# Three of six exponentials read from their PSUM bank, and a new order of work on VectorE, ScalarE and GpSimd

## The chip, the cores and the metric

One core of a Trainium2 chip runs the whole program. The metric is the device time of one execution in microseconds (us), median of several runs. On the core five engines run side by side, each with its own list of instructions in a fixed order: TensorE (PE in the profile, its weight loads PEld), VectorE (DVE), ScalarE (ACT), GpSimd (POOL) and SyncE (SP), which issues DMAs. They order each other only through semaphores: an instruction adds to one when it is done, and another engine waits until it has reached a count.

## What is computed

The reference is a decoder of two layers over 16 sequences of 256 tokens with 256 features: differential attention, cross attention, a mixture of experts, then a state-space block, causal cross attention and a feed-forward block with low-rank additions. After each comes a residual sum and a layer normalisation. Only the state-space block is touched:

```
zxbcdt = einsum('bld,ed->ble', x, in_proj_w)                 # z, x, B, C and dt per token
xBC    = silu(conv over 4 tokens (x, B, C) + conv_b)
dt     = softplus(dt + dt_bias);  A = -exp(A_log)
step:    state = state * exp(A * dt_t) + (x_t * dt_t) B_t;   y_t = state . C_t     # 8 heads
y      = (y + x * D) * silu(z)
y      = y * rsqrt(mean(y * y) + eps) * norm_w
out    = layernorm(x + y @ out_proj_w)
```

## The kernel before

`state_space` handles one sequence of 256 tokens in each step `n`, and the loop `STEPS` runs from -7 to 16, so that several sequences are in flight: in step n the block's core runs for sequence n, the output of sequence n-1 is finished, and sequences n+4, n+5 and n+7 are normalised, summed from the experts' outputs and gathered. The input projection is made for two sequences at a time (a pair), six of its eleven units in even steps and five in odd ones, through two PSUM banks (`in_ps`). So even and odd steps differ, and each engine has a list of its own for each, written out by hand.

The scan over tokens is done as matrices. For each sequence there are three blocks of 128 x 128 tokens and eight heads, which makes six units `u` of four heads (`u // 2` is the block). For each:

- `exponents(n, u)` on TensorE sums the decays into one of two PSUM banks, `e_ps[u % 2]` (two matmuls, of the high and the low part of the rows);
- `decays(n, u)` on ScalarE (line 2670) takes the exponential and writes it to `mat[:, u]` in SBUF;
- `matrices(eng, n, u)` (line 2827) multiplies `mat[:, u]` by the masked products `gm` of B and C, in place. VectorE does units 0, 2 and 4, GpSimd 1, 3 and 5;
- `mix(n, blk)` on TensorE multiplies the matrices with the rows `xdt` and `xdt_tail`. Its first half needs VectorE's three units, the second GpSimd's.

TensorE may write a bank again for `exponents(n, u + 2)` when `decays(n, u)` has read it: it waits for `decay_ready`. The same banks take the turned rows of the next sequence in `to_rows`, which VectorE's `scaled_rows` (line 2955) reads before the next step's exponents.

Other names that the steps below use: `masked_products` makes `gm` (line 2939, PSUM times a constant); `taps` are the convolution's three later taps on VectorE (line 2893, three instructions a unit), after ScalarE's `first_tap`; they free a bank of `in_ps`. `high_terms` (line 2930) and GpSimd's `low_terms` (line 3127) make the rows that the next exponents sum, `rhs_hi` and `rhs_lo`. `sum_experts` (lines 2867 and 2874, then moments) adds what the experts made of a sequence that comes five steps later; GpSimd's `scale_x` makes a scale and a shift of its moments in four small instructions, and ScalarE's `normalize_x` applies them a step later. `mean_squares` (line 2962) takes the mean square of y, GpSimd's `scale_rows` (line 3120) its inverse root, `residual` (line 2971) uses that; `row_moments`, GpSimd's `scale_y` (lines 3097 to 3102) and ScalarE's `normalize_y` finish the sequence. `skip_terms`, `gated` (line 3002), ScalarE's `upper_y` and `square_y` and GpSimd's `split_y` (line 3137) lead to TensorE's `output` in the next step. `gather` (line 3089) issues four indirect DMAs from GpSimd. `copy_steps` takes the dt rows out of their bank on ScalarE for TensorE's `turn_steps`.

## Time and profile before

| | us |
|---|---|
| median of 3 runs (2669.08 to 2676.38) | 2672.24 |
| the profiled execution | 2671.63 |
| its span, first to last instruction | 2669.9 |
| steps 4 and 5 of the state-space stage, from 1749.5 us on | 50.0 |
| mean granted TensorE clock, share of full speed | 0.937 |

Over the span TensorE was busy for 88%, its weight loads 74%, VectorE 73%, GpSimd 61% and ScalarE 53%. The state-space stage with all 16 sequences lies between about 1650 and 2050 us. A row of a timeline tells the start, the length, the engine, the line, the output and the inputs; `x2` are two instructions in one row, and a bracket holds the engine's idle time before it and what ended that. Rows of consecutive instructions overlap by about 0.1 us, since the end of one is written while the next begins.

### The profile page before, as it was taken

The numbers are of one execution on the slowest core, as the hardware profiler recorded it, in microseconds if no ns is written. First come the engines' busy times: TensorE is split into PE (matmuls) and PEld (weight loads), VectorE is DVE, ScalarE is ACT, GpSimd is POOL, SyncE is SP. The second block draws the span as 40 slices with busy tenths as digits, with TensorE's granted clock in tenths as the row PEclk, the third lists the DMA queues.
The fourth block names the chain that finished last, engine by engine and source line by source line (L and its number), as shares of the span: only waits on it lengthen the run. The fifth ranks groups of instructions, "written<-read, shape, count | busy, mean of one in ns | idle before, by whom it ended". The sixth has DMA issues, their size and how long they took to land. (4 is left out here: it accounts for less than half of the span.)

```text
span 2669.9 us, 63255 instructions
## 1 busy us (share of the span) xinstructions
PE 2341.5 (88%) x23480; PEld 1968.6 (74%) x23480; DVE 1950.1 (73%) x3223; ACT 1423.5 (53%) x2223; POOL 1619.4 (61%) x1937
## 2 busy tenths in 40 slices
PE   5999999997799877998999965988995899987998
PEld 4677777775566656998999964777774666756998
DVE  2677777776589872646888857999984588875776
ACT  2566666664466652335666544655652466653333
POOL 3667666764467751275666656777764587863443
PEclk9899999999899987999999987998996799988999
DMA  8566666551889841146666652111002887841111
GB/s 205 131 159 159 160 145 158 153 120 43 245 216 229 219 111 36 52 138 204 224 228 226 230 175 64 41 48 32 21 13 85 213 225 208 224 105 41 53 54 52
DMA packets 227288, 363.44 MB, mean 136 GB/s; under 512 B 51968, under 2 KB 156416, under 8 KB 219520
## 3 DMA queue, kind: packets, MB, share of 16 engines
q1 hardware_dynamic: 207392, 281.32, 39.7%
q0 software_dynamic: 17376, 78.13, 8.6%
q8 instruction: 143, 2.34, 0.4%
q10 hardware_dynamic: 2304, 1.05, 0.2%
q14 instruction: 73, 0.60, 0.1%
HBM read 231.72 MB, written 133.69 MB: 137 GB/s over the span
## 5 line engine op out<-in xcount | busy, mean ns | idle before, releaser
L1369 ACT ACTIVATE self_probs<-self_score_ps 128x768 f32<-128x768 f32 x256 | 208.7, 815 | 183.9 <-PE self_score_ps L1271 182.0
L1585 POOL TENSOR_SCALAR_AFFINE_SELECT self_probs<-self_probs 128x512 f32<-128x512 f32 x256 | 169.5, 663 | 158.6 <-ACT self_probs L1369 158.6
L1506 DVE TENSOR_REDUCE self_neg_max<-self_max_ps 128x2 f32<-128x256 f32 x256 | 108.1, 422 | 165.1 <-PE self_max_ps L88 165.1
L647 ACT ACTIVATE cross_probs<-cross_score_ps 128x1024 f32<-128x1024 f32 x128 | 131.2, 1025 | 101.6 <-PE cross_score_ps L545 100.0
L745 DVE TENSOR_REDUCE cross_neg_max<-cross_max_ps 128x4 f32<-128x1024 f32 x128 | 154.9, 1212 | 39.1 <-PE cross_max_ps L524 39.0
L1507 DVE TENSOR_REDUCE self_neg_max<-self_max_ps 128x2 f32<-128x512 f32 x256 | 174.5, 682 | 0.0
L2297 POOL TENSOR_TENSOR moee_h_lo<-moee_h,moee_h_hi 128x512 fp32r<-128x512 f32 x78 | 112.5, 1442 | 92.3 <-ACT moee_h_hi L2034 91.6
L739 DVE TENSOR_REDUCE causal_block_max<-causal_max_ps 128x6 f32<-128x768 f32 x128 | 120.9, 946 | 56.4 <-PE causal_max_ps L88 55.9
L3592 POOL TENSOR_TENSOR ffn_g_lo<-ffn_g_full,ffn_g_hi 128x512 fp32r<-128x512 f32 x64 | 82.1, 1283 | 129.2 <-ACT ffn_g_hi L3478 116.9
L2034 ACT ACTIVATE moee_h_hi<-moee_h 128x512 fp32r<-128x512 f32 x110 | 69.6, 632 | 163.2 <-DVE moee_h L2200 163.2
L647 ACT ACTIVATE causal_probs<-causal_score_ps 128x768 f32<-128x768 f32 x128 | 103.6, 809 | 99.2 <-PE causal_score_ps L545 99.0
L79 PE MATMUL moee_g_ps<-moee_x_hi,moee_in_hi 128*128 128x256 f32 x440 | 131.3, 298 | 10.0 <-DVE moee_x_lo L2187 5.8
L1271 PE MATMUL self_score_ps<-self_q_stack,self_k_stack 49*128 49x128 f32 (+1 forms) x1024 | 129.0, 330 | 10.0 <-ACT self_probs L1369 6.4
L2200 DVE TENSOR_TENSOR moee_h<-moee_u_ps,moee_silu 128x512 f32<-128x512 f32 x110 | 75.5, 686 | 82.0 <-PE moee_u_ps L81 77.4
L2240 POOL DMA_INDIRECT x_tiles<-kept_x,moek_slot x64 | 65.8, 1029 | 107.1 <-issue 104.1
L79 PE MATMUL moee_y_ps<-moee_out_hi,moee_h_hi 128*128 128x256 f32 x440 | 125.4, 285 | 0.7 <-DVE moee_out_lo L2152 0.7
L81 PE MATMUL moee_g_ps<-moee_x_hi,moee_in_lo 128*128 128x256 f32 x440 | 125.7, 286 | 0.0
L79 PE MATMUL moee_u_ps<-moee_x_hi,moee_in_hi 128*128 128x256 f32 x440 | 125.7, 286 | 0.0
L80 PE MATMUL moee_g_ps<-moee_x_lo,moee_in_hi 128*128 128x256 f32 x440 | 125.7, 286 | 0.0
L80 PE MATMUL moee_u_ps<-moee_x_lo,moee_in_hi 128*128 128x256 f32 x440 | 125.1, 284 | 0.0
L81 PE MATMUL moee_u_ps<-moee_x_hi,moee_in_lo 128*128 128x256 f32 x440 | 125.1, 284 | 0.0
L81 PE MATMUL moee_y_ps<-moee_out_hi,moee_h_lo 128*128 128x256 f32 x440 | 124.9, 284 | 0.0
(507 smaller groups left out, 9479.9 us busy)
## 6 DMA issues: line engine op xcount, KB each, us to landing
self_q<-self_q_split SPq DMA_DIRECT2D x48, 512.0 KB, 3.5
self_q_raw<-self_q SPq DMA_DIRECT2D x32, 768.0 KB, 8.2
cross_stacks<-cross_qk SPq DMA_DIRECT2D x64, 384.0 KB, 6.4
causal_stacks<-causal_qk SPq DMA_DIRECT2D x64, 384.0 KB, 6.4
moe_y_tiles<-lasting_y_out SPq DMA_DIRECT2D x55, 256.0 KB, 2.5
mid<-lasting_y_out SPq DMA_DIRECT2D x48, 256.0 KB, 2.2
x_tiles<-zeros SPq DMA_DIRECT2D x16, 624.0 KB, 5.5
moee_xT<-x_tiles SPq DMA_DIRECT2D x39, 256.0 KB, 7.3
```

The source lines that it names most:

```text
L79: pe.matmul(out, a[0], b[0], start=start, stop=False, **kw)
L80: pe.matmul(out, a[0], b[1], start=False, stop=False, **kw)
L81: return pe.matmul(out, a[1], b[0], start=False, stop=stop, **kw)
L647: nc.scalar.activation(probs[i // 2][:, a, :, lo:], score_ps[:, :, lo:], ACT.Exp, scale=HD ** -0.5).then_inc(prob_ready, 1)
L739: last = dve.tensor_reduce(block_max[:, :, col % 4, :], bank[:, :, 0:3 * P].rearrange("p a (j t) -> p a j t", t=P), AX.X, ALU.max, negate= ...
L745: last = dve.tensor_reduce(neg_max[p][:, tile, :, col % 4, :], bank[:].rearrange("p a (q k) -> p a q k", q=QT), AX.X, ALU.max, negate=True)
L1271: last = pe.matmul(score_ps[:, ab, j * S + k * P:(j + 1) * S], k_stack[p][rows, tile, k * P:(k + 1) * P], q_stack[rows, 4 * tile + c, k * P:],
L1369: nc.scalar.activation(probs[g % 4][:, a, :, P:], score_ps[:, :, P:], ACT.Exp, scale=HD ** -0.5).then_inc(prob_ready, 1)
L1506: dve.tensor_reduce(neg_max[:, tile, :, c, 0:1], bank[:, :, 0:P], AX.X, ALU.max, negate=True)
L1507: dve.tensor_reduce(neg_max[:, tile, :, c, 1:2], bank[:, :, S:2 * S], AX.X, ALU.max, negate=True).then_inc(max_kept, 1)
L1585: pool.affine_select(diagonal, diagonal, [[0, 2], [0, 2], [1, P]], ALU.is_ge, zero, base=0, channel_multiplier=-1).then_inc(prob_masked, 1)
L2297: pool.tensor_tensor(h_lo[p][f][:].rearrange("p j s -> p (j s)"), h[f][:], h_hi[p][f][:].bitcast(F32).rearrange("p j s -> p (j s)"), ALU.s ...
```

## The change

Three things change in `state_space`; nothing else does.

1. `decays` of units 0, 2 and 4 write the exponential back into the bank `e_ps[0]` that they read, and VectorE's `matrices` reads it from there. So the bank is free only when VectorE has multiplied: `exponents` 2 and 4, and `to_rows` for its first half, wait for `low_mat_ready` in place of `decay_ready`. The wait for the earlier `mix`, which protects `mat`, moves to the first writer.
2. The order on VectorE. Even steps: the multiplications go between the taps, `sum_experts` from the start behind multiplication 4, `residual` to right behind `mean_squares`, `high_terms` behind `gated`. Odd steps: multiplications 0 and 2 follow `masked_products`, then `tail_rows`, taps, multiplication 4, `sum_experts`, `mean_squares`, `residual`.
3. ScalarE in even steps: `decays` 1 follows `decays` 0, `normalize_x` comes behind `decays` 3, `copy_steps` ahead of `square_y`. GpSimd in odd steps: `scale_x` comes behind multiplication 5, ahead of `low_terms`, not behind the gather.

```diff
             def exponents(n, u):
-                if u >= 2:
+                if u in (2, 4):
+                    pe.wait_ge(low_mat_ready, 3 * n + u // 2)
+                elif u >= 2:
                     pe.wait_ge(decay_ready, 6 * n + u - 1)
...
             def to_rows(b):
                 for q in range(QT):
-                    if b:
-                        pe.wait_ge(decay_ready, 6 * b - 1 + q)
+                    if b and q == 0:
+                        pe.wait_ge(low_mat_ready, 3 * b)
+                    elif b:
+                        pe.wait_ge(decay_ready, 6 * b)
...
             def decays(n, u):
                 act.wait_ge(e_done, 6 * n + u + 1)
-                if u == 0 and n:
+                if u == 1 and n:
                     act.wait_ge(ssm_done, 2 * n)
-                nc.scalar.activation(mat[:, u, :, :].rearrange("p h t -> p (h t)"), e_ps[u % 2][:],
-                                     ACT.Exp).then_inc(decay_ready, 1)
+                dst = mat[:, u, :, :].rearrange("p h t -> p (h t)") if u % 2 else e_ps[0][:]
+                nc.scalar.activation(dst, e_ps[u % 2][:], ACT.Exp).then_inc(decay_ready, 1)
...
         def matrices(eng, n, u, ready):
             eng.wait_ge(decay_ready, 6 * n + u + 1)
             eng.wait_ge(gm_ready, n + 1)
-            eng.tensor_tensor(mat[:, u, :, :], mat[:, u, :, :],
+            src = mat[:, u, :, :] if u % 2 else e_ps[0][:].rearrange("p (h t) -> p h t", t=P)
+            if u == 0 and n:
+                eng.wait_ge(ssm_done, 2 * n)
+            eng.tensor_tensor(mat[:, u, :, :], src,
                               gm[:, u // 2, :].unsqueeze(1).broadcast_to([P, 4, P]), ALU.mult).then_inc(ready, 1)
...
         # ScalarE, even steps
                     if now:
                         decays(n, 0)
+                        decays(n, 1)
                     first_tap(n, 1)
-                    if real(n + 4):
-                        normalize_x(n + 4)
                     if now:
-                        decays(n, 1)
                         decays(n, 2)
                         tails(n)
                         decays(n, 3)
+                    if real(n + 4):
+                        normalize_x(n + 4)
...
                     if now:
                         upper_y(n)
+                    copy_steps(n)
+                    if now:
                         square_y(n)
                     if late:
                         normalize_y(n - 1)
-                    copy_steps(n)
...
         # VectorE, even steps
+                    if now:
+                        masked_products(n)
+                        matrices(dve, n, 0, low_mat_ready)
+                    taps(n, 0)
+                    if now:
+                        matrices(dve, n, 2, low_mat_ready)
+                    taps(n, 1)
+                    if now:
+                        tail_rows(n)
+                        matrices(dve, n, 4, low_mat_ready)
                     if real(n + 5) and n != -2:
                         sum_experts(n + 5)
-                    if now:
-                        masked_products(n)
-                    taps(n, 0)
-                    taps(n, 1)
-                    if now:
-                        matrices(dve, n, 0, low_mat_ready)
-                        matrices(dve, n, 2, low_mat_ready)
-                        tail_rows(n)
-                    if n >= 0 and soon:
-                        high_terms(n + 1)
-                    if now:
-                        matrices(dve, n, 4, low_mat_ready)
                     taps(n, 2)
                     if late:
                         mean_squares(n - 1)
-                    taps(n, 3)
+                        residual(n - 1)
                     if now:
                         skip_terms(n, 0)
-                    if late:
-                        residual(n - 1)
+                    taps(n, 3)
                     if now:
                         skip_terms(n, 1)
                         gated(n)
+                    if n >= 0 and soon:
+                        high_terms(n + 1)
...
         # VectorE, odd steps
                         masked_products(n)
-                    if real(n + 5):
-                        sum_experts(n + 5)
-                    if now:
                         matrices(dve, n, 0, low_mat_ready)
                         matrices(dve, n, 2, low_mat_ready)
                         tail_rows(n)
                     taps(n, 0)
+                    if now:
+                        matrices(dve, n, 4, low_mat_ready)
+                    if real(n + 5):
+                        sum_experts(n + 5)
                     if late:
                         mean_squares(n - 1)
-                    if now:
-                        matrices(dve, n, 4, low_mat_ready)
-                    if late:
                         residual(n - 1)
...
         # GpSimd, odd steps
                         matrices(pool, n, 5, high_mat_ready)
-                    if n == -5:
-                        scale_x(n + 5)
-                    if n == -3:
+                    if n >= -5 and real(n + 5):
                         scale_x(n + 5)
...
                         gather(n + 7)
-                    if n >= -1 and real(n + 5):
-                        scale_x(n + 5)
```

## Rows read from the trace of the kernel before

**Rows 1.** Windows: stretch and length, busy time (instructions) of each engine, PEclk, DMA.
```profile
1749.50:1775.00 25.50, 20.98 (x148) 17.38 (x148) 24.71 (x41) 11.53 (x20) 17.23 (x22) 0.93 0.04 13
1775.00:1799.50 24.50, 22.80 (x160) 19.72 (x160) 23.28 (x50) 18.70 (x29) 21.20 (x19) 1.00 0.25 74
...
1902.00:1995.00 93.00, 85.25 (x594) 71.83 (x592) 83.12 (x139) 55.86 (x88) 57.26 (x54) 0.94 0.04 12
```

**Rows 2.** Groups by line on VectorE, 1652.8 to 1925.7: busy us, mean ns.
```profile
L2827 DVE TENSOR_TENSOR ssm_mat<-ssm_mat,ssm_gm 128x512 f32<-128x512 f32 x33 | 36.4, 1129 | 0.0
...
L2947 DVE TENSOR_TENSOR ssm_xdt_tail<-ssm_xdt,ssm_tail 128x512 f32<-128x512 f32 x11 | 11.8, 1076 | 0.0
```

**Rows 3.** Two lines over the whole span: ns minimum/median/maximum, first and last start.
```profile
L2827 DVE TENSOR_TENSOR ssm_mat<-ssm_mat,ssm_gm x48: 656/790/2387, 1658.3 to 2021.6; 128x512 f32<-128x512 f32 x48
...
L2955 DVE TENSOR_TENSOR ssm_xdt<-ssm_e_ps,ssm_dt x32: 656/681/691, 1646.1 to 2011.7; 128x512 f32<-128x512 f32 x32
```

**Rows 4.** Timeline of VectorE in steps 4 and 5: start, us, instruction.
```profile
1754.32 2.59 DVE L2827 TENSOR_TENSOR ssm_mat<-ssm_mat,ssm_gm 128x512 f32<-128x512 f32 x2
1756.84 1.77 DVE L2947 TENSOR_TENSOR ssm_xdt_tail<-ssm_xdt,ssm_tail 128x512 f32<-128x512 f32 x1
...
1763.62 0.15 DVE L2962 TENSOR_SCALAR ssm_ms<-ssm_g_ps 128x2 f32<-128x2 f32 x1
...
1775.46 1.91 DVE L2867 SCALAR_TENSOR_TENSOR ssm_y_shared<-ssm_y_routed,moek_weight,ssm_y_shared 128x256 f32<-128x256 f32 x2
...
1783.35 2.37 DVE L2827 TENSOR_TENSOR ssm_mat<-ssm_mat,ssm_gm 128x512 f32<-128x512 f32 x1
1786.40 0.88 DVE L2971 SCALAR_TENSOR_TENSOR lasting_y_out<-ssm_xT_ps,ssm_row_scale,ssm_x 128x256 f32<-128x256 f32 x2 [0.68 <-issue]
...
1793.76 3.01 DVE L2930 TENSOR_TENSOR ssm_rhs_hi<-ssm_triang,ssm_a_hi 128x1024 fp32r<-128x1024 f32 x2
1796.69 0.87 DVE L2867 SCALAR_TENSOR_TENSOR ssm_y_shared<-ssm_y_routed,moek_weight,ssm_y_shared 128x256 f32<-128x256 f32 x2
...
1799.47 0.52 DVE L2939 TENSOR_TENSOR ssm_gm<-ssm_g_ps,ssm_triang 128x384 f32<-128x384 f32 x1
```

**Rows 5.** Timeline of GpSimd in the same steps.
```profile
1754.64 3.42 POOL L2827 TENSOR_TENSOR ssm_mat<-ssm_mat,ssm_gm 128x512 f32<-128x512 f32 x2
...
1763.85 0.69 POOL L3120 TENSOR_TENSOR ssm_row_scale<-ssm_ms,ssm_neg_half 128x2 f32<-128x2 f32 x1 [1.23 <-DVE ssm_ms L2962]
...
1771.14 0.23 POOL L3097 TENSOR_SCALAR ssm_var<-ssm_mv 128x2 f32<-128x2 f32 x1 [2.89 <-issue]
...
1772.54 0.20 POOL L3102 TENSOR_TENSOR ssm_shift<-ssm_low,ssm_rstd 128x2 f32<-128x2 f32 x1
...
1777.25 1.09 POOL L3089 DMA_INDIRECT ssm_y_routed<-moe_y_tiles,moek_slot  x1 [0.17 <-issue]
...
1782.62 2.54 POOL L2827 TENSOR_TENSOR ssm_mat<-ssm_mat,ssm_gm 128x512 f32<-128x512 f32 x2
...
1788.46 1.90 POOL L3127 TENSOR_TENSOR ssm_rhs_lo<-ssm_triang,ssm_a_lo 128x1024 fp32r<-128x1024 f32 x1 [0.90 <-DVE ssm_a_lo L2924]
```

**Rows 6.** Timeline of ScalarE, end of step 5.
```profile
1792.74 1.09 ACT L2759 ACTIVATE lasting_y_out<-lasting_y_out,ssm_shift,ssm_rstd 128x256 f32<-128x256 f32 x2 [0.67 <-POOL ssm_shift L3102]
...
1798.70 0.60 ACT L2670 ACTIVATE ssm_mat<-ssm_e_ps 128x512 f32<-128x512 f32 x1
```

**Rows 7.** Timeline of TensorE in step 4, around its longest wait.
```profile
1749.54 0.39 PE L2526 MATMUL ssm_e_ps<-ssm_rhs_hi,ssm_one_r 128*128 128x512 f32 x1
1749.77 0.39 PE L2527 MATMUL ssm_e_ps<-ssm_rhs_lo,ssm_one_r 128*128 128x512 f32 x1
1753.87 0.50 PE L2526 MATMUL ssm_e_ps<-ssm_rhs_hi,ssm_one_r 128*128 128x512 f32 x1 [3.72 <-ACT ssm_mat L2670]
...
1755.53 0.63 PE L80 MATMUL ssm_in_ps<-ssm_x_lo,ssm_w_hi 128*128 128x512 f32 x1
```

**Rows 8.** Window of step 13, columns as in rows 1.
```profile
1970.00:1976.90 6.90, 6.25 (x18) 4.97 (x19) 3.28 (x6) 3.35 (x10) 3.62 (x4) 0.51 0.11 38
```

## What I predicted, before the kernel ran

> **What bounds the kernel now.** I read the table of busy times by stretch first. In the state-space stage two steps, one even and one odd, take 50.0 us (25.5 + 24.5), and VectorE's records cover 47.99 of them, more than TensorE's 43.78 and GpSimd's 38.43 [rows 1]. Towards the end, when `sum_experts` has no batches left, VectorE is busy for 83.12 of 93.0 us and is no longer the only limit [rows 1]. The groups by line, read next, say how much of VectorE's time is work. Up to step 11 the 33 multiplications of `matrices` average 1129 ns and `xdt_tail` 1076 [rows 2], while the quickest multiplication took 656 ns and the slowest 2387 [rows 3]. The timelines show why: at 1754.32 two of VectorE's multiplications take 2.59 us while two of GpSimd's, which started at 1754.64, take 3.42 [rows 4, 5]; at 1783.35 one of VectorE's takes 2.37 us behind two of GpSimd's from 1782.62 [rows 4, 5]. They take turns. An instruction of VectorE with two SBUF inputs stretches when GpSimd computes beside it; `xdt`, with one input in PSUM and one in SBUF, never does (656 to 691 ns in 32) [rows 3].
>
> For one pair I subtract the stretching. In the pair of rows 4, even step: the two multiplications and `xdt_tail` cost 2.4 us over their free times. Odd step: `y_shared` 1.0 (1.91 for two against 0.87), the third multiplication 1.7, `rhs_hi` 0.65 (3.01 against about 2.35). That is 5.8 us. With 1.1 us of waits, 0.68 of it before `residual` at 1786.40 [rows 4] (the rest of its 2.0 idle is pauses of 0.04 that stay), about 43.1 us of work are left of 50.0.
>
> **The change, part by part.**
>
> *Exponentials 0, 2 and 4 stay in their bank.* ScalarE's instructions are as many as before; VectorE's multiplication gets one PSUM and one SBUF input. No row shows a multiplication of this form on these tiles; nearest is `xdt`, the same shape with one PSUM input, 0.68 us [rows 3]. I take 0.68. The stretch of the multiplications goes: 33 x (1129 - 680) ns = 14.8 us up to step 11, 2.7 per pair; 3.0 in the pair above (1.3 + 1.7). An exponential that writes PSUM isn't in the trace either; it stands off VectorE's path by its own length, so I bound it by plus or minus 0.1 us on 0.60 [rows 6], and take 0.
>
> The Trainium skill, Perfetto Trace Analysis, section Optimizing Scalar/DVE Operations, speaks against this part: it gives VectorE about 60 ns of access per instruction on SBUF and 125 on PSUM. By it 48 multiplications would be 3.1 us dearer (an estimate from that page). The rows do not show it: the quickest `xdt` from PSUM and the quickest multiplication from SBUF both took 656 ns [rows 3].
>
> *The price: bank 0 is free only when VectorE has multiplied.* TensorE's `exponents` 2 and 4 now wait for `low_mat_ready`. Behind them in TensorE's queue stand the projections. In odd steps the new order puts multiplication 2 straight behind multiplication 0. VectorE then waits for a round trip: its 0.68 us, a hop of 0.15, two matmuls (0.23 from the first to the second, 0.39 for that: 0.63 with the hop) [rows 7], one exponential of 0.60 and hops of 0.1: 2.15 us from start to start, of which multiplication 0 fills 0.59. **New idle: 1.57 per pair.** A first tap that ScalarE does behind the same exponentials adds 0.4. In even steps `taps` stand between the multiplications and cover it.
>
> *`sum_experts` moves.* It is 2.78 us (1796.69 to 1799.47) [rows 4], once in every step. At the start of an even step it filled VectorE until exponential 0 of that step was there. In the new order `masked_products` and multiplication 0 come first. When is that exponential there? I count from `mean_squares` of the odd step. GpSimd: `scale_rows` 0.7 (with its hop 0.9), `mat` 5 1.3, then `scale_x`, which the change puts ahead of `low_terms`: four small ones like those from 1771.14 to 1772.74, 1.6; `low_terms` 1.9; `scale_y` 1.6 [rows 5]. That is 7.4, or 8.4 where VectorE's `gated`, with two SBUF inputs, stands in the way. ScalarE from `normalize_y` to the end of exponential 0: 1792.74 to 1799.30, 6.6 back to back [rows 6]. Sum 14.0 to 15.0. VectorE's own work from `mean_squares` to that multiplication is 11.3, with a wait that comes next. **New idle: 2.0 to 2.7 per pair** (2.0 if `rhs_hi` is stretched by the second `low_terms`, which then costs nothing).
>
> *`residual` right behind `mean_squares`, in both steps.* It needs `row_scale` of GpSimd. In rows 4 and 5 `ms` starts at 1763.62, GpSimd's answer ends at 1764.54; before, taps or a multiplication lay between. **New idle: 0.9 + 0.85 per pair** (0.7 of it was there already in the odd step, as part of the 1.1 taken out above).
>
> *What still collides.* `sum_experts` of the odd step comes now behind multiplication 4. GpSimd's gather takes 5.4 us (1777.25 to 1782.62) and its two multiplications follow [rows 5]. By the new order I place the end of the gather and the start of `sum_experts` within 2 us of each other, so its four two-input instructions meet `mat` 1 and 3 of GpSimd: 1.0 to 2.3 us, 0 at best. `xdt_tail` of the even step meets `mat` 3: 0.4; the small `dt`: 0.3. I take 2.2. `rhs_hi` of the even step, now behind `gated`, finds GpSimd idle.
>
> *TensorE.* `rhs_hi` and `row_moments` now stand ahead of `scaled_rows`, so TensorE waits about 2.9 us more before the exponents of the odd step; in the even step it waits 1.2 + 1.7 for the round trips, in place of the 3.72 behind `normalize_x` [rows 7], which goes as that step moves. After 3.72 us idle the trace shows 0.63 us matmuls in place of 0.39 [rows 7], and after two waits of 1.44 near the end the granted clock was 0.51 for 6.9 us, its 1.2 GHz level [rows 8]. If the odd step's waits do that too, the round trip and `taps` start 1.25 later; in the even step up to 1.85. Between 0 and 3.1; I take 0.7, since part of it is hidden by the collision that then ends earlier.
>
> *No effect taken:* `copy_steps` earlier (0.6 us of ScalarE that TensorE waited for, no longer on the path), `normalize_x` later in even steps (its input was late anyway, its reader comes after `mix`).
>
> **The sum.** New pair: 43.1 + 1.57 + 0.4 + 2.4 + 1.75 + 2.2 + 0.7 = 52.1, against 50.0: +2.1 for each of the five pairs from step 0 to 9: +11. Bounds: 43.1 + 5.7 + 0.4 = 49.2 to 43.1 + 6.4 + 3.0 + 3.1 = 55.6, or -4 to +28 over five pairs. Steps 10 to 13 have `sum_experts` once; there VectorE was idle for 10 us already [rows 1], so lost stretching and new waits about cancel: 0, between -3 and +3. Steps 14 and 15 hang on TensorE's chain: two banks that come free 0.75 later in each step (3.0) and `scaled_rows` 2.3 later, less 1 of stretching: +4, between +2 and +6. Together +15. No other stage is touched, and the next one starts when this one's rows are stored. The profiled execution was 2671.6 us with a span of 2669.9, 0.6 below the median of 2672.2; so 2672 + 15 = **2687**.
>
> **The rivals.**
> 1. *Faster: the exponential is there in time.* If GpSimd and ScalarE answer `mean_squares` within 11.3 us and not 14, VectorE never waits at the even start, and the saved stretching is what counts: 43.1 + 1.57 + 0.4 + 1.75 + 0.4 = 47.2, or -2.8 a pair, with the last steps about 2660. For it speaks that VectorE is the fullest engine [rows 1]; against it that ScalarE's 6.6 alone are back to back [rows 6].
> 2. *No change: the waits are as new, but GpSimd's gather keeps out of `sum_experts`' way.* 49.2 to 50.3 a pair: 2670 to 2678. A shift of 2 us in the phase is enough.
> 3. *Slower still: TensorE falls to 1.2 GHz in each step* [rows 7, 8]. 2.4 us a pair more than the forecast: 2699.
> 4. *It does not do what it says*: multiplications from PSUM that stretch as well would leave 2.7 a pair in: about 2700. `xdt` speaks against it [rows 3].
>
> **How the numbers follow.** A measurement of this kernel tells about 0.3%, 8 us, from no change. Forecast (2680 to 2694) 0.41; faster 0.16; no change 0.22; slower still 0.19; the last 0.02. Below 2658 I leave about 0.07, above 2710 about 0.08, where bounds of several terms add up. Faster by over 0.3%: 0.15; within: 0.23; slower: 0.62.
>
> **What would show it.** VectorE's multiplications at 0.66 to 0.69 us, all of them. An idle 1.5 us on VectorE before multiplication 2 of odd steps, released by ScalarE; 2 to 3 us before multiplication 0 of even steps, also by ScalarE; 0.9 before `residual`, by GpSimd. `y_shared` and `x` of odd steps stretched beside GpSimd's multiplications. VectorE busy for less than 46 us of a pair. If instead a pair takes 47 and the idle before multiplication 0 is under 0.5 us, my count of GpSimd's and ScalarE's answer is wrong, and with it the sign.

## The result and the profile after

The changed kernel takes 2718.02 us (median of 4 runs, 2713.84 to 2719.44) against 2671.66 for the kernel before (median of 4), a ratio of 1.0169 with a 95% interval of 1.0154 to 1.0183. It is slower, as forecast, but by 46 us and not by 15, and above the forecast's range. The profiled execution took 2719.44 us with a span of 2717.7, 47.8 more than the span before. All of it lies in the state-space stage: from the first `gm` to GpSimd's last `shift`, 1.1 us before the stage's last instruction ends, it took 391.7 us before and 440.0 after; what follows took 625.4 and 624.4.

The first view to read is the table of windows, cut within 0.4 us of the starts of `gm`. Columns as in rows 1: stretch and length, busy us (instructions) of PE, PEld, DVE, ACT and POOL, granted clock, DMA share, GB/s. Of after: the first pair, steps 2 to 9, then steps 4 and 5 alone, steps 10 and 11, 12 and 13, and the end:

```profile
1653.30:1709.00 55.70, 41.89 (x266) 33.46 (x265) 50.09 (x81) 28.71 (x46) 37.19 (x35) 0.91 0.12 34
...
1708.97:1927.92 218.95, 185.95 (x1225) 153.21 (x1224) 187.77 (x348) 120.36 (x193) 150.84 (x161) 0.92 0.13 37
...
1763.76:1793.44 29.68, 24.89 (x157) 19.91 (x156) 26.53 (x48) 13.97 (x23) 17.57 (x21) 0.88 0.08 21
1793.44:1818.80 25.36, 22.25 (x152) 19.03 (x151) 20.73 (x41) 16.17 (x26) 20.35 (x21) 0.94 0.21 61
1927.80:1979.00 51.20, 46.05 (x311) 38.16 (x311) 42.02 (x79) 31.30 (x50) 28.98 (x30) 0.93 0.03 11
1979.00:2029.50 50.50, 43.49 (x294) 35.59 (x292) 38.41 (x67) 26.92 (x42) 26.20 (x25) 0.93 0.04 12
2029.50:2093.30 63.80, 45.57 (x250) 40.91 (x250) 21.79 (x49) 13.38 (x23) 24.21 (x28) 0.65 0.03 9
```

The same cuts of before that rows 1 do not have:

```profile
1652.90:1699.50 46.60, 40.92 (x277) 34.35 (x276) 44.03 (x80) 30.84 (x48) 34.66 (x31) 0.96 0.12 36
...
1699.40:1902.00 202.60, 177.58 (x1226) 149.96 (x1225) 192.27 (x350) 120.83 (x192) 154.19 (x162) 0.95 0.13 39
...
1902.00:1946.50 44.50, 41.83 (x301) 35.81 (x300) 42.41 (x72) 28.66 (x47) 28.92 (x30) 0.96 0.04 13
1946.50:1995.00 48.50, 43.42 (x295) 36.03 (x293) 40.72 (x69) 27.20 (x42) 28.33 (x25) 0.93 0.04 12
1995.00:2044.50 49.50, 34.94 (x250) 30.95 (x250) 26.16 (x49) 13.21 (x23) 24.98 (x28) 0.77 0.03 11
```

| stretch | before | after | difference | forecast |
|---|---|---|---|---|
| steps 0 and 1 | 46.6 | 55.7 | +9.1 | +2.1 |
| steps 2 to 9 (four pairs) | 202.6 | 219.0 | +16.4 | +8.4 |
| steps 10 to 13 | 93.0 | 101.6 | +8.6 | 0 |
| steps 14, 15 and the end | 49.5 | 63.8 | +14.3 | +4 |

In steps 2 to 9 VectorE's busy time fell by 4.5 us, from 192.27 to 187.77, and its idle time rose by 20.9, from 10.3 to 31.2. So the change bought 1.1 us of work per pair and paid 5.2 of idle time. The groups by line say where, first after, then before, both over those eight steps on VectorE (busy us, mean ns | idle time before them and its releasers):

```profile
L2938 DVE TENSOR_TENSOR ssm_rhs_hi<-ssm_triang,ssm_a_hi 128x1024 fp32r<-128x1024 f32 x16 | 25.3, 1625 | 0.0
L2835 DVE TENSOR_TENSOR ssm_mat<-ssm_e_ps,ssm_gm 128x512 f32<-128x512 f32 x24 | 16.5, 686 | 17.2 <-ACT ssm_e_ps L2675 16.8
L2875 DVE SCALAR_TENSOR_TENSOR ssm_y_shared<-ssm_y_routed,moek_weight,ssm_y_shared 128x256 f32<-128x256 f32 x16 | 11.9, 784 | 0.0
L2955 DVE TENSOR_TENSOR ssm_xdt_tail<-ssm_xdt,ssm_tail 128x512 f32<-128x512 f32 x8 | 10.1, 1260 | 0.0
...
L2979 DVE SCALAR_TENSOR_TENSOR lasting_y_out<-ssm_xT_ps,ssm_row_scale,ssm_x 128x256 f32<-128x256 f32 x16 | 7.0, 480 | 7.1 <-issue 5.3 <-POOL ssm_row_scale L3125 1.8
```

```profile
L2827 DVE TENSOR_TENSOR ssm_mat<-ssm_mat,ssm_gm 128x512 f32<-128x512 f32 x24 | 27.6, 1178 | 0.0
L2930 DVE TENSOR_TENSOR ssm_rhs_hi<-ssm_triang,ssm_a_hi 128x1024 fp32r<-128x1024 f32 x16 | 21.5, 1382 | 1.6 <-PE ssm_e_ps L2527 1.6
L2867 DVE SCALAR_TENSOR_TENSOR ssm_y_shared<-ssm_y_routed,moek_weight,ssm_y_shared 128x256 f32<-128x256 f32 x16 | 11.2, 736 | 0.0
```

The multiplications do what part 1 promised: 1178 ns became 686, 11.1 us saved in four pairs. But 17.2 us of idle time now stand before them, 7.1 before `residual` (2.7 before the change), and `rhs_hi` gave 3.8 us of the saving back (1382 to 1625 ns). The timeline of VectorE in steps 4 and 5 shows each place once:

```profile
1751.06 0.13 DVE L2970 TENSOR_SCALAR ssm_ms<-ssm_g_ps 128x2 f32<-128x2 f32 x1
...
1759.42 4.05 DVE L2938 TENSOR_TENSOR ssm_rhs_hi<-ssm_triang,ssm_a_hi 128x1024 fp32r<-128x1024 f32 x2
1763.76 0.56 DVE L2947 TENSOR_TENSOR ssm_gm<-ssm_g_ps,ssm_triang 128x384 f32<-128x384 f32 x1 [0.28 <-PE ssm_g_ps L2513]
1766.04 0.69 DVE L2835 TENSOR_TENSOR ssm_mat<-ssm_e_ps,ssm_gm 128x512 f32<-128x512 f32 x1 [1.72 <-ACT ssm_e_ps L2675]
...
1771.68 2.10 DVE L2955 TENSOR_TENSOR ssm_xdt_tail<-ssm_xdt,ssm_tail 128x512 f32<-128x512 f32 x1
...
1794.08 0.69 DVE L2835 TENSOR_TENSOR ssm_mat<-ssm_e_ps,ssm_gm 128x512 f32<-128x512 f32 x1
1797.27 0.69 DVE L2835 TENSOR_TENSOR ssm_mat<-ssm_e_ps,ssm_gm 128x512 f32<-128x512 f32 x1 [2.50 <-ACT ssm_e_ps L2675]
...
1801.65 2.21 DVE L2875 SCALAR_TENSOR_TENSOR ssm_y_shared<-ssm_y_routed,moek_weight,ssm_y_shared 128x256 f32<-128x256 f32 x2
...
1807.08 0.88 DVE L2979 SCALAR_TENSOR_TENSOR lasting_y_out<-ssm_xT_ps,ssm_row_scale,ssm_x 128x256 f32<-128x256 f32 x2 [0.89 <-POOL ssm_row_scale L3125]
```

GpSimd's timeline has the partner of each stretched row: `rhs_lo` beside `rhs_hi`, its two multiplications beside `xdt_tail`, and again beside `y_shared`:

```profile
1759.41 2.99 POOL L3132 TENSOR_TENSOR ssm_rhs_lo<-ssm_triang,ssm_a_lo 128x1024 fp32r<-128x1024 f32 x1
...
1770.70 2.51 POOL L2835 TENSOR_TENSOR ssm_mat<-ssm_mat,ssm_gm 128x512 f32<-128x512 f32 x2
...
1800.65 2.52 POOL L2835 TENSOR_TENSOR ssm_mat<-ssm_mat,ssm_gm 128x512 f32<-128x512 f32 x2
```

### The profile page after: what moved, and what is told of

Same layout as the page of the kernel before. It is cut to its first block and busy times, and to the rows that moved or that the text cites. A ratio compares the mean times of both kernels' runs of the same rounds, so it can differ in the third digit from the quotient of the medians.

```text
span 2717.7 us, 63255 instructions
## 1 busy us (share of the span) xinstructions
PE 2356.4 (87%) x23480; PEld 1974.3 (73%) x23480; DVE 1947.2 (72%) x3223; ACT 1423.7 (52%) x2223; POOL 1613.4 (59%) x1937
## 5 line engine op out<-in xcount | busy, mean ns | idle before, releaser
L80 PE MATMUL moee_y_ps<-moee_out_lo,moee_h_hi 128*128 128x256 f32 x440 | 125.0, 284 | 0.0
```

The source lines that it names most:

```text
L80: pe.matmul(out, a[0], b[1], start=False, stop=False, **kw)
```

## Experiments

Ten kernels ran, in three groups; times are compared as ratios to runs of the kernel before on the same chip, and the stage time is that of the one profiled run. e8 and e9 have the same code up to step 11, and their pairs in steps 2 to 9 differ by 0.5 us, so smaller differences are not read. The median of the kernel before was 2671.3 us beside e1 to e4, 2677.8 beside e5 to e8 and 2672.1 beside e9 and e10; where a theory's range in us is close, the ratio is the better measure. In the expectations the theories have names. In the first four, *Waits* is the forecast's own (new waits of VectorE at the start of even steps, in the odd round trip and before `residual`); *Bank* says that holding `e_ps[0]` until VectorE has multiplied is what costs; *Clock*, that TensorE's 1.2 GHz level is. In the next four, *Chain* is the answer of GpSimd and ScalarE to `mean_squares`, *VectorE* its collisions and covers. In the last one *Order* says that the order of work is the whole gain.

| kernel | ratio [95%] | stage | pair, steps 2 to 9 | steps 10 to 13 | end |
|---|---|---|---|---|---|
| before | 1 | 391.7 | 50.7 | 93.0 | 49.5 |
| after | 1.0169 [1.0154, 1.0183] | 440.0 | 54.7 | 101.6 | 63.8 |
| e1 bank part alone | 1.0136 [1.0119, 1.0153] | 426.8 | 55.3 | 96.5 | 57.4 |
| e2 order alone | 1.0239 [1.0222, 1.0256] | 455.3 | 61.9 | 101.6 | 55.2 |
| e3 even `sum_experts` first | 1.0163 [1.0144, 1.0182] | 435.3 | 55.9 | 100.9 | 63.7 |
| e4 odd `sum_experts` between | 1.0098 [1.0077, 1.0118] | 416.7 | 51.2 | 101.2 | 63.6 |
| e5 `scale_x` back | 1.0147 [1.0122, 1.0171] | 437.2 | 54.5 | 102.1 | 64.0 |
| e6 `high_terms` back | 1.0118 [1.0092, 1.0144] | 428.0 | 55.6 | 98.4 | 53.9 |
| e7 TensorE kept busy | 1.0092 [1.0064, 1.0121] | 422.1 | 55.1 | 98.3 | 51.7 |
| e8 combined | 0.9967 [0.9954, 0.9980] | 386.8 | 47.5 | 88.8 | 61.0 |
| e9 combined, end kept busy | 0.9951 [0.9933, 0.9969] | 378.3 | 48.0 | 90.3 | 49.9 |
| e10 combined, without the bank | 0.9991 [0.9976, 1.0005] | 389.1 | 49.5 | 91.1 | 53.7 |

**The two parts apart.** e1 is the kernel before with the four edits of part 1 alone; e2 is the changed kernel without them.

```diff
 # e2, against the changed kernel (e1 is the reverse, against before); one of four places
...
-                dst = mat[:, u, :, :].rearrange("p h t -> p (h t)") if u % 2 else e_ps[0][:]
-                nc.scalar.activation(dst, e_ps[u % 2][:], ACT.Exp).then_inc(decay_ready, 1)
+                nc.scalar.activation(mat[:, u, :, :].rearrange("p h t -> p (h t)"), e_ps[u % 2][:],
+                                     ACT.Exp).then_inc(decay_ready, 1)
...
```

> The first part of the change alone, in the old order of work: exponentials 0, 2 and 4 stay in their bank, TensorE waits for the multiplication. Three theories. Waits: the loss comes from the new waits of VectorE, most of them made by the order; here the multiplications stop stretching (-2.7 us a pair), but multiplication 2 stands right behind 0 in both kinds of step and waits for a round trip of 1.6 to 2.5 us each: 2670 to 2685. Bank: holding the bank is what costs, whatever the order: 2700 or more. Clock: what costs is TensorE at 1.2 GHz, which follows wherever it waits long; it waits longer for the bank here, as VectorE multiplies after two units of taps: 2685 to 2700.

> The second part alone: the new order on VectorE, ScalarE and GpSimd, with the exponentials in SBUF as before. Waits: the wait for the round trip of the odd step goes (-2.5 us a pair), the stretch of the multiplications beside GpSimd returns (+2 to 3), the idle start of the even step and the wait before residual stay: 2700 to 2718. Bank: the order alone is harmless: 2668 to 2680. Clock: TensorE's long wait before the exponents of the odd step stays, so most of the loss does: 2700 to 2712.

Each part alone loses. e1 came out where Bank put it (2706 us), e2 above all three ranges (2736). The order costs 64 us of stage without the bank, the bank 35 in the old order, both together 48: in the new order the bank part gains 15. With the exponentials in SBUF the new order lets VectorE's multiplications meet GpSimd's far more than the old one, as the group of e2 over steps 2 to 9 shows, and the wait before them is there without any hold on the bank:

```profile
L2828 DVE TENSOR_TENSOR ssm_mat<-ssm_mat,ssm_gm 128x512 f32<-128x512 f32 x24 | 46.2, 1924 | 14.5 <-ACT ssm_mat L2670 14.1
```

In e1 the loss has another form: VectorE's old order multiplies late, and TensorE waits 9.1 us per pair at `e_ps` for VectorE's multiplication. In TensorE's waits over steps 2 to 9 (us in total, times, longest) it is the first line:

```profile
PE ssm_e_ps L2528 <- DVE ssm_mat L2834: 36.4, 8, 5.6
```

So Bank is true of the old order and not of the new one.

**Covering one wait at a time.**

```diff
 # e3, even steps
+                    if real(n + 5) and n != -2:
+                        sum_experts(n + 5)
                     if now:
                         masked_products(n)
...
                         matrices(dve, n, 4, low_mat_ready)
-                    if real(n + 5) and n != -2:
-                        sum_experts(n + 5)
...
 # e4, odd steps
                         matrices(dve, n, 0, low_mat_ready)
+                    if real(n + 5):
+                        sum_experts(n + 5)
+                    if now:
                         matrices(dve, n, 2, low_mat_ready)
...
                         matrices(dve, n, 4, low_mat_ready)
-                    if real(n + 5):
-                        sum_experts(n + 5)
```

> The changed kernel with sum_experts of the even step back at the step's start, where VectorE waits 2.0 us for exponential 0. Waits: 2.8 us of work fill that wait, about -2 us in each of 5.5 pairs: 2704 to 2709. Bank and Clock: TensorE is not touched, so no gain: 2714 to 2720.

> The changed kernel with sum_experts of the odd step between multiplications 0 and 2, where VectorE waits 2.5 us for the round trip. Waits: the wait is filled and sum_experts no longer meets GpSimd's multiplications (1.3 us): -3 to -3.8 us a pair, 2697 to 2703. Bank: the same round trip, now hidden: the same as Waits. Clock: TensorE's waits are as long, no gain: 2712 to 2720.

e4 takes 3.5 us off each pair of steps 2 to 9, 8.5 off the first pair, and nothing in steps 10 to 13, where there is no odd `sum_experts` to move: VectorE does the sums while the exponential makes its round trip, and they no longer meet GpSimd's multiplications (`y_shared` 784 to 586 ns in those steps, `xdt_tail` 1260 to 851). It took 2695 us, just under the range of Waits. e3 missed the range of Waits (2717 us): it fills the wait at the even start in the same way, but its pairs of steps 2 to 9 are not shorter (55.9); only the first is (47.0). The idle time that left the multiplications (4.3 to 2.8 us a pair) came back before `ms`, `yz` and `residual`, 1.8, 0.95 and 0.5 more, where VectorE waits for TensorE. One wait filled only shows the next.

**The chain, the collision and the clock.**

```diff
 # e5, GpSimd, odd steps: scale_x as before the change
-                    if n >= -5 and real(n + 5):
+                    if n == -5:
+                        scale_x(n + 5)
+                    if n == -3:
                         scale_x(n + 5)
...
                         gather(n + 7)
+                    if n >= -1 and real(n + 5):
+                        scale_x(n + 5)
...
 # e6, VectorE, even steps
                         matrices(dve, n, 4, low_mat_ready)
+                    if n >= 0 and soon:
+                        high_terms(n + 1)
...
                         gated(n)
-                    if n >= 0 and soon:
-                        high_terms(n + 1)
...
 # e7, TensorE: multiplications of constants into a bank that is idle then; nobody reads them
+            def keep_busy(n, count, bank=None):
+                pe.wait_ge(yd_ready, 2 * n)
+                for _ in range(count):
+                    pe.matmul((y_ps[1] if bank is None else bank)[:], w_hi[:, 0, 0:P], w_hi[:, 0, 0:512],
+                              start=True, stop=True)
...
                         state_products(n)
+                        keep_busy(n, 10 if n < 15 else 18)
                         exponents(n, 0)
...
```

> The changed kernel with GpSimd's scale_x of the odd step back behind the gather. Theory Chain: a pair's length is set by the answer of GpSimd and ScalarE from mean_squares of an odd step to exponential 0 of the next even one (15.0 us measured, 1.6 of it scale_x), then by TensorE's work from there; filling VectorE's wait could not help. It expects 1.6 us less in each of 5.5 pairs: 2707 to 2710. Theory Clock: what costs is TensorE at 1.2 GHz; its waits stay, so 2714 to 2720. Theory VectorE (its own work and waits are the bound): no gain, 2714 to 2720, or a loss where normalize_x then comes late.

> The changed kernel with high_terms of the even step back ahead of the output work (behind multiplication 4), so that scaled_rows comes 2.3 us earlier and TensorE's wait of 2.85 us before the exponents of the odd step nearly goes. Chain: the same work on VectorE, the odd step not longer or shorter where VectorE is full: -1 us a pair, -4 in the last two steps: 2706 to 2714. Clock: TensorE doesn't fall in the odd step, the round trip falls from 2.5 to 1.6 us: -2 us a pair and -6 in the last steps: 2698 to 2706. VectorE: nothing, 2714 to 2720.

> The changed kernel with matmuls on constants added on TensorE where it waits: 10 ahead of the odd step's exponents, 3 and 4 around exponents 2 and 3 of the even step, more in steps 14 and 15; their results are never read. They fit into the waits of 2.85, 0.8 and 1.0 us, so they cost under 0.5 us a pair. Clock: the time at 1.2 GHz in steps 2 to 9 falls from 8.5 us a pair to under 3 and the time by 8 to 20 us: 2698 to 2710. Chain: the clock rises, but the pair hangs on waits of other engines, so only the round trip gains, 0.4 to 0.9 us a pair: 2708 to 2716. VectorE: 2714 to 2722.

e5: the chain to the even exponential 0 became 1.0 us shorter (14.4 to 13.4 from `mean_squares` to that exponential), and `rhs_hi` no longer met the second `rhs_lo` (1625 to 1382 ns). The sums took it back (`y_shared` 784 to 918 ns, `x` 538 to 731): 0.2 us a pair are left, less than is read here. Its time, 2716 us or 1.0147, does not decide between the theories.

e6 makes the pairs of steps 2 to 9 no shorter (55.6): `rhs_hi` stretches less (1625 to 1324 ns), but `y_shared` went from 784 to 1180 ns and `gated` from 1219 to 1585. It shortens the end by 10 us, with TensorE at its 1.2 GHz level for 66.3 us of the stage in place of 102.4. That `scaled_rows` comes earlier for the last sequence is the likely reason (TensorE's wait for it in the end fell from 4.2 us to 1.9); no run shows it apart. The time, 2707 us or 1.0118, fits Chain by the one and Clock by the other.

e7 raises the clock and leaves the order alone; more of its multiplications stand around exponents 2 and 3 of even steps and of step 15. With TensorE kept busy it ran at its 1.2 GHz level for 30.7 us of the stage, not for 102.4, and the round trip in odd steps fell from 3.19 us (1794.08 to 1797.27 in the rows above) to 2.20, close to the forecast's 2.15. The end became 12.1 us shorter, the first pair 4.0 and steps 10 to 13 3.3, but steps 2 to 9 stayed at 55.1 a pair. There the idle time before the multiplications fell by 5 us in four pairs, and `y_shared` beside GpSimd (784 to 1155 ns) and the wait before `gm` (1.1 to 5.5 us) took it back. Groups over steps 2 to 9, and the end (columns as above):

```profile
L2848 DVE TENSOR_TENSOR ssm_mat<-ssm_e_ps,ssm_gm 128x512 f32<-128x512 f32 x24 | 16.5, 687 | 12.2 <-ACT ssm_e_ps L2688 11.8
L2888 DVE SCALAR_TENSOR_TENSOR ssm_y_shared<-ssm_y_routed,moek_weight,ssm_y_shared 128x256 f32<-128x256 f32 x16 | 17.8, 1155 | 0.0
L2960 DVE TENSOR_TENSOR ssm_gm<-ssm_g_ps,ssm_triang 128x384 f32<-128x384 f32 x8 | 4.4, 554 | 5.5 <-PE ssm_g_ps L2513 5.5
```

```profile
2028.30:2080.00 51.70, 40.55 (x288) 35.35 (x286) 22.70 (x49) 13.01 (x23) 24.17 (x28) 0.90 0.03 11
```

So the clock makes the end long (0.65 granted there after the change, 0.90 here), and a higher clock alone does not make steps 2 to 9 shorter. The extra multiplications stand in TensorE's queue too, so e7 may give back less than the clock costs.

**All covers together.** e8 keeps part 1 and ScalarE's new order. Even steps: `sum_experts` first, multiplications between the taps, `high_terms` behind multiplication 4, `residual` behind `skip_terms` 0 and a unit of taps. Odd steps: `sum_experts` between multiplications 0 and 2. GpSimd: `scale_x` behind the gather.

```diff
 # e8, beside the edits of e3, e4, e5 and e6
                         mean_squares(n - 1)
-                        residual(n - 1)
+                    taps(n, 3)
                     if now:
                         skip_terms(n, 0)
-                    taps(n, 3)
+                    if late:
+                        residual(n - 1)
                     if now:
                         skip_terms(n, 1)
```

> The exponentials from their bank and ScalarE's new order, but sum_experts of the even step at its start, that of the odd step between multiplications 0 and 2, high_terms behind multiplication 4, residual of the even step behind skip_terms 0, and scale_x behind the gather. All three theories expect it faster than the changed kernel; Chain: each answer of another engine is now covered by work, the multiplications don't stretch: 48 to 50 us a pair, 2660 to 2680. Clock: fewer waits of TensorE, the same. VectorE: 43.1 us of work and the collisions of sum_experts, 2655 to 2675.

e8 is faster than both kernels, if by little: 2668.72 us, ratio 0.9967. All theories had expected it. Its groups over steps 2 to 9:

```profile
L2938 DVE TENSOR_TENSOR ssm_rhs_hi<-ssm_triang,ssm_a_hi 128x1024 fp32r<-128x1024 f32 x16 | 23.4, 1502 | 0.0
L2835 DVE TENSOR_TENSOR ssm_mat<-ssm_e_ps,ssm_gm 128x512 f32<-128x512 f32 x24 | 16.3, 681 | 0.7
L2875 DVE SCALAR_TENSOR_TENSOR ssm_y_shared<-ssm_y_routed,moek_weight,ssm_y_shared 128x256 f32<-128x256 f32 x16 | 8.8, 589 | 0.0
...
L2955 DVE TENSOR_TENSOR ssm_xdt_tail<-ssm_xdt,ssm_tail 128x512 f32<-128x512 f32 x8 | 5.9, 740 | 0.0
```

The multiplications are as short as in the changed kernel (681 ns), and of the 17.2 us of idle time before them 0.7 are left. VectorE's waits that remain are for TensorE's answers in odd steps (0.96 us a pair before `ms`, 1.36 before `residual`). The windows of e8 for steps 4 and 5 and for the end:

```profile
1747.40:1794.90 47.50, 42.77 (x306) 35.45 (x306) 44.00 (x88) 30.31 (x49) 37.80 (x41) 1.00 0.16 46
1978.30:2039.30 61.00, 44.39 (x250) 39.74 (x250) 22.66 (x49) 13.39 (x23) 24.89 (x28) 0.66 0.03 9
```

In the steps the clock is now 1.00, at the end still 0.66. Two more kernels follow from that: e9 is e8 with the idle multiplications of e7 from step 12 on, e10 is e8 without part 1.

```diff
 # e9, against e8; e10 has e2's edit against e8
             def keep_busy(n, count, bank=None):
+                if n < 12:
+                    return
...
```

> The combined order of work of the run before (exponentials in their bank, sum_experts ahead of gm in even steps and between multiplications 0 and 2 in odd ones, high_terms behind multiplication 4, residual of even steps behind skip_terms 0, scale_x behind the gather), with TensorE kept busy in its waits of steps 12 to 15 by multiplications of constants that nobody reads. Clock: the last two steps took 61.0 us there with TensorE at its 1.2 GHz level, and 51.7 in the changed kernel once TensorE was kept busy; here they take 50 to 53, steps 2 to 9 stay at 47.5 a pair, and the ratio to before goes from 0.9967 to 0.992 to 0.994. Chain: the last two steps are long because banks come free late and not because of the clock; they stay above 58, ratio 0.996 to 0.999.

> The combined order of work, but all six exponentials written to SBUF as before the change, and TensorE waiting for the exponential alone. Bank: with the waits covered, the bank part saves the stretching of VectorE's three multiplications (2.7 us a pair before) less some 0.6 us of the round trip that is still there; without it the multiplications average 1100 to 1300 ns again and a pair of steps 2 to 9 takes 49 to 51 in place of 47.5; ratio 1.000 to 1.008. Order: the covered order is the whole gain and the bank held until VectorE has multiplied costs as much as it saves; a pair takes 46.5 to 48, ratio 0.993 to 0.998.

e9: the end took 49.9 us at a granted clock of 0.89, and its stage is the shortest of all, 378.3. The end is just under Clock's 50 to 53; the ratio, 0.9951, lies between the two theories' ranges. The time, 2657.87 us, is the best of all, but the intervals of e8 and e9 overlap, and the profiled run of e9 was 8.9 us longer behind the stage than that of e8. So the end is shown to shrink by 11 us, and the gain in the whole time is measured less surely. e10: without the bank the multiplications average 1257 ns again and a pair takes 2.0 us more than in e8, both as Bank had it, and the end takes 7.3 us less (61.0 against 53.7). The ends of e9 and e10, and e10's group over steps 2 to 9:

```profile
1985.20:2035.20 50.00, 40.02 (x288) 35.53 (x286) 23.52 (x49) 13.10 (x23) 24.25 (x28) 0.89 0.03 11
...
1989.17:2042.87 53.70, 39.16 (x250) 35.05 (x250) 26.27 (x49) 13.26 (x23) 25.13 (x28) 0.74 0.03 11
...
L2828 DVE TENSOR_TENSOR ssm_mat<-ssm_mat,ssm_gm 128x512 f32<-128x512 f32 x24 | 30.2, 1257 | 1.7 <-ACT ssm_mat L2670 0.9
```

What the bank part is worth in the whole time is not shown. The ratios differ by 0.2%, but the medians of e8 and e10 are 2668.72 and 2668.62 us, and the difference comes from the kernel before, which took 2677.8 beside e8 and 2672.1 beside e10. The stage is 2.3 us shorter with it.

## Why the prediction was right in its direction and wrong in its size

The steps that failed are the end (10.3 us of the missing 34), steps 10 to 13 (8.6), steps 2 to 9 (8.0) and the first pair (7.0).

**Right: the multiplications.** All 48 took 677 to 693 ns; the forecast took 0.68, with 2.7 us a pair saved. Measured: 11.1 us in four pairs, 2.8 each. Rival 4 is out. The Trainium skill, Perfetto Trace Analysis, section Optimizing Scalar/DVE Operations, gives about 125 ns of access on PSUM and 60 on SBUF; by an estimate from that they would be 65 ns dearer. The trace shows less: the quickest went from 656 ns [rows 3] to 677, a third of that, and `xdt_tail`, the same shape with both inputs in SBUF, took 684 undisturbed (mean in e2) where the multiplications took 687.

**Right: the waits, in kind and place.** `residual` waits 0.89 in each step (1.78 a pair; forecast 1.75); the profile names GpSimd for two of the eight and nothing for six of the same length. Multiplication 2 of odd steps waits for ScalarE, 2.50 us; 1.5 of it is the round trip, and the rest TensorE at 1.2 GHz, since e7 brought the round trip to 2.20. The forecast had 1.57, 0.4 for a first tap and 0.7 for the clock, 2.67 together; measured 2.9 (4.3 before multiplications less 1.72, and 0.36 before the taps).

**Wrong: the even start, by 1.3 us a pair.** The chain was counted rightly: 14.0 to 15.0 us from `mean_squares` to multiplication 0, measured 15.0 (1751.06 to 1766.04). But from 11.3 us of VectorE's own work that leaves 2.7 to 3.7, and the forecast put 2.0 to 2.7 and took 2.4, saying that `rhs_hi`, if stretched, "then costs nothing": it left out the upper end of its own chain. It does stretch, 4.05 us for two against 2.35 free, and 2.0 of idle time come on top (0.28 and 1.72 in the rows above). The two together are the 3.7 that the chain's upper end leaves.

**Wrong: "What still collides", by some 0.6.** The forecast had 2.2 a pair. `y_shared` and `x` lost 1.45 (mean 784 and 538 ns, against 472 where nothing collides, in e10, and 482 before; four of each in a pair), `xdt_tail` 1.15 (1260 ns against 684, two in a pair), `dt` 0.2: 2.8. The places were right, the share of `xdt_tail` was 0.4 and should have been three times that. With 0.25 at the round trip and 0.65 because the pair of rows 4 was shorter (50.0) than the mean of steps 2 to 9 (50.7), 52.1 + 1.3 + 0.6 + 0.25 + 0.65 = 54.9, against 54.7 measured. So VectorE's busy time in steps 4 and 5 is 47.3 us, where the forecast said under 46.

**Wrong: the first pair counted like the others.** +9.1, not +2.1. VectorE was busy there for 44.03 us before, for 50.09 after: the sums and `xdt_tail` ran free of GpSimd before, and now they do not. In step 0 of the changed kernel the whole collision stands in three rows:

```profile
1660.47 3.10 DVE L2955 TENSOR_TENSOR ssm_xdt_tail<-ssm_xdt,ssm_tail 128x512 f32<-128x512 f32 x1
...
1664.09 3.12 DVE L2875 SCALAR_TENSOR_TENSOR ssm_y_shared<-ssm_y_routed,moek_weight,ssm_y_shared 128x256 f32<-128x256 f32 x2
1667.25 2.39 DVE L2882 SCALAR_TENSOR_TENSOR ssm_x<-ssm_y_routed,moek_weight,ssm_y_shared 128x256 f32<-128x256 f32 x2
```

They take 8.6 us in place of about 2.4. It is a matter of phase: in e4, which leaves the even steps alone, the same three ran free in step 0 (0.68, 0.87 and 0.88 us).

**Wrong: steps 10 to 13 at zero.** The forecast read one window of 93 us, saw 10 us of idle time on VectorE [rows 1] and let it absorb the new waits. Cut in two, that window says something else: the idle time before was 2.1 us in steps 10 and 11 (42.41 of 44.5) and 7.8 in 12 and 13. In steps 10 and 11 there was nothing to absorb the waits, and after the change 9.2 us are idle there (2.55 before multiplication 2, 2.2 before `residual`, 1.7 before multiplication 0). In 12 and 13 there was room, and yet they grew by 2.0. Idle time elsewhere in a window covers nothing.

**Wrong: the end, and there it was the clock.** +14.3 where +4 was forecast. The waits came out nearly as counted: TensorE's waits at `e_ps` in that stretch rose from 5.9 us to 9.5, by 3.6. The rest is its clock: the same 250 instructions kept it busy for 45.57 us in place of 34.94, 10.6 more, at a granted 0.65 against 0.77 (44.4 us of the stretch at the 1.2 GHz level against 23.2). e3, e4 and e5 have the same end within 0.3 us, and e7, with TensorE kept busy, takes 12.1 off it. The forecast had 0.7 us a pair for the clock, and 2.4 more as a rival, but no term for it at the end, where rows 8 had shown 0.51 already in step 13: the place was wrong, not the mechanism.

**Rivals 1 and 2** fell with the phase: the exponential is not there in time (15.0 us), and the gather ends at 1800.65 while `sum_experts` starts at 1801.65, so it meets GpSimd's multiplications (1800.65 to 1803.17). Rival 3 has its part, but in the last steps. The stage's difference was forecast at 14.5 and is 48.3; the missing 34 are 7.0 in the first pair, 8.0 in steps 2 to 9 (the 1.3, 0.6 and 0.25 above make 8.6 in four pairs), 8.6 in steps 10 to 13 and 10.3 at the end.

What stays open: the end with the bank part, 61.0 us in e8 and 53.7 in e10. The traces split the 7.3 us: 2.1 are TensorE's waits at `e_ps`, for VectorE's multiplications in e8 (5.5) and for ScalarE's exponentials in e10 (3.4), and 5.2 are the same 250 instructions at a lower clock (44.39 busy against 39.16). But waits alone do not tell the clock. In the end TensorE waits about as long in e6 as in e8 (13.8 and 13.7 us), and its clock is higher in e6:

```profile
2028.70:2082.60 53.90, 37.28 (x250) 32.90 (x250) 22.80 (x49) 13.39 (x23) 24.80 (x28) 0.73 0.03 10
```

Why, no run shows. Nor is the share of two parts that never ran alone: ScalarE's new order, and the move of `residual`. e3 to e6 add up to 1.6 us a pair in steps 2 to 9, and e8 gains 7.2; the rest is the later `residual` or what the covers do only together.

## What to carry to other kernels

When an order of work is changed by hand, price each wait by the work that will stand in it, and then ask what the second-latest input is: of e3 to e6, each of which removed one cause, only e4 shortened steps 2 to 9 by more than the 0.5 us a pair that two runs of the same code differ by, and the four together with a later `residual` took 7.2 us off a pair. In the others the collisions with GpSimd moved to another place. A piece of work with no urgent reader, as `sum_experts` here, belongs into the one gap that a round trip to another engine leaves. And idle time is read pair by pair: a window over two pairs hid that one of them had almost none.

## What the runs showed of the hardware

VectorE, with two inputs in SBUF, and GpSimd wait for each other's whole instructions. One `rhs_hi`, 1.21 us at its quickest, took 2.92 beside a `rhs_lo` that ran from 1759.41 to 1762.40. The turns need not alternate: the `xdt_tail` of 3.10 us in step 0 (0.68 free) waited for two of GpSimd's multiplications. GpSimd pays as well: a small scale instruction of 0.23 us took 1.17 beside `gated`, which took 1.21. The Trainium skill, SBUF — State Buffer, section Who interferes with whom, says that an instruction of VectorE with at most one SBUF input, outside its two-port modes, does not contend; the 48 multiplications at 677 to 693 ns agree.

```profile
1760.56 2.92 DVE L2938 TENSOR_TENSOR ssm_rhs_hi<-ssm_triang,ssm_a_hi 128x1024 fp32r<-128x1024 f32 x1
...
1660.51 2.51 POOL L2835 TENSOR_TENSOR ssm_mat<-ssm_mat,ssm_gm 128x512 f32<-128x512 f32 x2
...
1811.92 0.23 POOL L3102 TENSOR_SCALAR ssm_var<-ssm_mv 128x2 f32<-128x2 f32 x1
1812.22 1.17 POOL L3103 TENSOR_SCALAR ssm_low<-ssm_mv 128x2 f32<-128x2 f32 x1
```

On ScalarE an exponential from PSUM back into PSUM took 582 ns and into SBUF 592 (medians of 48 each), and each even step pays a table load of 1.28 us just before its first exponential, on the chain that VectorE waits for; the forecast had it inside its 6.6 us without a name:

```profile
1764.13 1.28 ACT L2675 ACT_TABLE_LOAD   x1
1765.42 0.58 ACT L2675 ACTIVATE ssm_e_ps<-ssm_e_ps 128x512 f32<-128x512 f32 x1
```
